# First layer's end on two engines: GpSimd finishes three heads while VectorE divides

## What is computed

```
e = exp(leaky_relu(s_src[src] + s_dst[dst], 0.2))
rowsum = segment_sum(e, src)
agg = segment_sum(e[:, None] * h[dst], src)
h_prime = agg / rowsum[:, None]
outs.append(elu(h_prime))        # once per head, four heads
x = x + mean(outs)
```

## Time and profile before

| | us |
|---|---|
| median of 3 runs | 4261.27 (4261.18 to 4268.39) |
| the profiled execution, device time | 4261.19 |
| its span in the trace | 4258.6 |
| VectorE busy over the span | 2922.2 |
| GpSimd busy over the span | 1967.2 |
| this stage, first of VectorE's wide instructions to the next layer's first | 1654.1 to 1828.1 |

### The profile page before, as it was taken

One profiled execution on the slowest core, in us unless ns is written; L12 is line 12 of the kernel. 1 busy time (PEld: TensorE's weight loads), 2 busy tenths in 40 slices (PEclk: granted clock), 3 DMA queues, 4 the chain that ended last, 5 costly groups with the idle time before them and its releaser, 6 DMA issues. The chain is left out here.

```text
span 4258.6 us, 43791 instructions
## 1 busy us (share of the span) xinstructions
PE 1503.5 (35%) x10631; PEld 933.2 (22%) x10631; DVE 2922.2 (69%) x5610; ACT 1413.3 (33%) x3645; POOL 1967.2 (46%) x2324
## 2 busy tenths in 40 slices
PE   3270201110000000000565541322221498999988
PEld 2150101110000000000222220111111386444444
DVE  5875599984678888988887866577878677132131
ACT  1442402111366567533011212344444553010011
POOL 0047778736777760002677771677777230000000
PEclk9995555555555555555887775555555799999999
DMA  3000000005776760000233332688887275868845
GB/s 143 16 21 1 4 1 1 1 1 157 200 196 190 196 170 0 0 0 19 60 91 101 101 91 60 208 258 261 257 260 236 61 204 180 331 225 277 279 144 194
DMA packets 215402, 553.60 MB, mean 130 GB/s; under 512 B 46178, under 2 KB 112412, under 8 KB 214405
## 3 DMA queue, kind: packets, MB, share of 16 engines
q0 software_dynamic: 99984, 272.83, 23.1%
q1 hardware_dynamic: 115188, 278.18, 19.2%
HBM read 485.70 MB, written 65.20 MB: 129 GB/s over the span
## 5 line engine op out<-in xcount | busy, mean ns | idle before, releaser
L2898 PE MATMUL fourth_bank<-fourth_tile,fourth_z 128*128 128x512 f16 (+1 forms) x2800 | 559.7, 362 | 19.8 <-DVEq L3059 10.1
L2257 POOL DMA_INDIRECT heads_got<-rec,heads_slot x416 | 482.3, 1159 | 134.7 <-issue 88.4
L1778 POOL DMA_INDIRECT sum_got<-rec,sum_slot x416 | 437.7, 1052 | 132.6 <-issue 68.8
L1103 POOL DMA_INDIRECT table<-edges_record,edges_place x391 | 419.8, 1074 | 123.7 <-POOL table_pause L264 107.4
L1374 POOL DMA_INDIRECT blend_got<-rec,blend_slot x416 | 401.9, 966 | 136.1 <-issue 123.7
L1474 PE MATMUL blend_count<-blend_mov,blend_stat 128*128 x1100 | 288.7, 406 | 231.6 <-DVE blend_stat L1429 213.3
L218 PE MATMUL edges_p_key<-kept_ident,edges_key_row 128*128 128x128 f32 x4 | 1.1, 427 | 981.6 <-DVEq L176 981.6
L2898 PEld LDWEIGHTS fourth_bank<-fourth_tile,fourth_z 128*128 128x128 f16 x2800 | 261.6, 99 | 311.6 <-issue 15.0
L1864 DVE TENSOR_TENSOR first_y<-first_y,sum_got 128x516 f32 x416 | 291.9, 702 | 33.3 <-DVE sum_got L1842 12.5
L2371 DVE TENSOR_TENSOR third_a_y<-third_a_y,heads_got 128x520 f32 x416 | 289.5, 696 | 1.3 <-DVE third_a_y L2371 0.2
L1428 DVE TENSOR_SCALAR blend_mov<-built_iota_low,built_low 128x800 f16 x550 | 248.7, 452 | 56.9 <-issue 47.9
(11 more groups left out here) (678 smaller groups left out, 4441.0 us busy)
## 6 DMA issues: line engine op xcount, KB each, us to landing
fourth_tile<-cs SPq DMA_DIRECT2D x100, 800.0 KB, 4.5
fourth_tile<-ct SPq DMA_DIRECT2D x100, 800.0 KB, 4.3
ct<-blend_cst SPq DMA_DIRECT2D x20, 1000.0 KB
heads_counts<-ct SPq DMA_DIRECT2D x25, 800.0 KB
cs<-heads_flipped SPq DMA_DIRECT2D x25, 800.0 KB, 5.4
attend_cnt<-ct SPq DMA_DIRECT2D x50, 256.0 KB, 3.0
sort_low_wide<-low SPq DMA_DIRECT2D x4, 3136.0 KB, 21.8
attend_cnt<-ct SPq DMA_DIRECT2D x25, 288.0 KB, 4.0
```

Of the source, the lines that this page charges most:

```text
L1103: pool.indirect_dma_start(table, bass.IndirectOffsetOnAxis(ap=K["place"][0:lanes, t:t + 1], axis=0), K["record"][0:lanes, t, :], None).the ...
L1778: pool.indirect_dma_start(got[:, t % (HELD * PART), :], None, rec_dram, bass.IndirectOffsetOnAxis(ap=slot[:, t:t + 1], axis=0)).then_inc(g ...
L2257: pool.indirect_dma_start(got[:, buf, r, :], None, rec_dram, bass.IndirectOffsetOnAxis(ap=slot[:, t:t + 1], axis=0)).then_inc(gathered[buf ...
L2898: last = pe.matmul(bank[m][:, 0:w], z2[s % 2][:, k, part, :], tile[:, n % RING, at:at + w], start=(k == 0 and part == 0), stop=(k == NB - ...
```

## The change

`finish_head` and the sum of heads 0 and 1 leave VectorE. GpSimd gets a block of its own in `finish_once`: for heads 0, 1 and 2 it waits for `lifted`, takes the maximum with zero in one instruction, adds `e` in a second, and behind head 1 it adds head 1 to head 0. Each of its instructions is awaited before the next. VectorE waits for `joined` and for `finished` once, ahead of the last head's three pieces. ScalarE's code is unchanged; its waits on `finished` are now for GpSimd.

```diff
-            def finish_head(k):
-
-                dve.wait_ge(lifted, k + 1)
-                step(dve.scalar_tensor_tensor(head(k), head(k), 0.0, e, ALU.max, ALU.add))
-                dve.sem_inc(finished, 1)
...
                 subtract_low(k)
                 correct(k)
-                if k >= 1:
-                    finish_head(k - 1)
-                if k == 2:
-                    step(dve.tensor_tensor(head(0), head(0), head(1), ALU.add))
+            dve.wait_ge(joined, 1)
+            dve.wait_ge(finished, heads - 1)
             for n, at in enumerate(thirds):
                 finish_last(n, at)
+
+        @block.gpsimd
+        def _(pool):
+            for k in range(heads - 1):
+                pool.wait_ge(lifted, k + 1)
+                pool.tensor_scalar(head(k), head(k), 0.0, None, ALU.max).then_inc(cut, 1)
+                pool.wait_ge(cut, k + 1)
+                pool.tensor_tensor(head(k), head(k), e, ALU.add).then_inc(finished, 1)
+                pool.wait_ge(finished, k + 1)
+                if k == 1:
+                    pool.tensor_tensor(head(0), head(0), head(1), ALU.add).then_inc(joined, 1)
+            pool.wait_ge(joined, 1)
```

More of the change, by code:

```diff
@@ L1897, in finish_once @@
         v, ready, estimated, split, products = (c.sem(n) for n in ("v", "ready", "estimated", "split", "products"))
-        subtracted, divided, lowered, lifted, finished = (c.sem(n) for n in ("subtracted", "divided", "lowered", "lifted", "finished"))
+        subtracted, divided, lowered, lifted = (c.sem(n) for n in ("subtracted", "divided", "lowered", "lifted"))
+        cut, finished, joined = c.sem("cut"), c.sem("finished"), c.sem("joined")
         x = K["x"][:, :, :]
```

## The result

The changed kernel takes 4291.76 us (median of 4 runs, 4289.76 to 4294.54) against 4261.23 for the kernel before (4 runs): ratio 1.0068, 95% interval 1.0051 to 1.0085, so 22 to 36 us slower. The forecast was 4284.1, range 4259 to 4302.

What follows compares the result with a forecast made beforehand. The stage was taken as one VectorE chain with its ScalarE helper ahead of it. GpSimd's holds of 37.3 us less 14.45 saved gave +22.85 us on the profiled 4261.19 or median 4261.27, forecast 4284.1, range 4259 to 4302.

Steps and rivals of the forecast that it cites:

- the step that decides: What VectorE does during GpSimd's instructions: each holds VectorE for its full length, 37.3 us in all; full hold 66%.
- the boundary forecast: Head 0's maximum on GpSimd waits for the VectorE instruction boundary at 1711.26, then runs to 1714.4.
- Head 2's hand-over: Head 2 lifted at about 1805, during head 3's high subtraction, some 26 us of VectorE's chain left; pair costs 10.1 us.
- The 14.45 us taken off the chain: Four instructions leave VectorE's chain in the stage: 3 x 3.64 + 3.53 = 14.45 us saved.
- The full length: VectorE's loss per GpSimd instruction, taken as that instruction's whole duration; lower end 0.07 us an instruction.
- The gather of 4.06 us: Earlier-stage GpSimd gather beside a two-input VectorE instruction, 4.06 us instead of 0.95; cited as evidence of the hold.
- No hold: Rival A: GpSimd runs beside VectorE for nothing, the whole 14.45 us is kept, 4246.8 us; chance 18%.
- a partial hold: Rival B: VectorE gets some turns between pieces of GpSimd's stream; at half of 37.3 us, +4.2, 4265.5; chance 12%.
- VectorE always wins the interface: Rival C: GpSimd waits until VectorE runs dry at head 3's low subtraction, then work is serial; 4285 us, chance 4%.
- The fourth rival: Rival D: a GpSimd instruction runs far slower than three passes; each further us on an addition costs 4; no chance given.
- the shortest cover of 15.7: From 1778.0 to 1793.7, 15.7 us for GpSimd's two instructions on head 2; a 10.1 us pair fits.
- The term that was mis-sized: GpSimd's instruction times: three maxima at 3.1 us and four additions at 7.0, 37.3 us in all.

Runs made afterwards that it cites:

- the first probe: Kernel before plus a block behind the first layer's end: GpSimd alone, then its additions beside five kinds of VectorE instruction; kernel time meaningless, VectorE stretched 13.4 us or nothing.
- the serial kernel: Changed kernel with VectorE told to wait while GpSimd works, so nothing overlaps but ScalarE: 4300.71 us, ratio 1.0083, stage 210.34 us.
- the probes: Two kernels, the kernel before plus a block timing GpSimd instructions, alone or also beside VectorE; maximum alone 8.31 us, multiply-and-add 2.86.

## Why the prediction was right, and where its size was off

**Mechanism.** Right in the step that decides: VectorE lost GpSimd's instructions nearly whole, seven times, and for head 0 at the boundary forecast (the maximum was granted at 1710.45; on the axis of before, 0.8 us later, that is the predicted 1711.26). GpSimd got its turn between VectorE instructions 0.03 us apart, and one VectorE instruction passed between two of GpSimd's. ScalarE never became late. Head 2's hand-over met the last high subtraction of head 3, as forecast, though 7.5 us later than 1805 because of the longer holds ahead of it. The 26 us of VectorE's chain said to be left there count in the pair's own hold; without it 15.7 us were left, still enough for both holds to count in full. The 14.45 us taken off the chain closed the sum of every experiment that had them.

The full length was a guess of the prediction's all the same, and the rows did not show it. The gather of 4.06 us was held by VectorE, but it did not hold VectorE: L553, which started 0.82 us before the gather ended, stands at 3.49 us. That GpSimd's arithmetic holds VectorE, and for how long, was first shown by the profile after. The Trainium skill (SBUF — State Buffer, Who interferes with whom) has the exclusion for the whole instruction and exempts VectorE instructions with one SBUF input outside the two-port mode; the first probe agrees with both halves, 13.4 us against nothing.

**Rivals.** No hold (4246.8) and a partial hold (4265.5) fell with the profile, and the serial kernel closed the matter: 2.94 us is all that overlap is worth. That VectorE always wins the interface fell too: VectorE never ran dry and has no idle time at head 3's low subtraction. The fourth rival wanted an instruction far slower than three passes, 8.9 us; none was, with 8.3 us at most. But the maximum came near that, and a pair took 8.16 + 6.8 = 15.0 us, just inside the shortest cover of 15.7. The sign hung on the hold alone.

**The term that was mis-sized** is what GpSimd's instructions take. The maximum was put at 3.1 us, by the rate of a select that reads and writes one stream, with 5.8 as upper end. It takes 8.15 to 8.3. By VectorE's stretches the three maxima cost 7.98 + 7.98 + 7.74 = 23.7 us instead of 9.3. The four additions cost 6.60 + 6.64 + 5.43 + 5.43 = 24.1 instead of 28: 7.0 was right for two of them (6.93 and 6.96 alone), two are of the quick pairing (5.86). Together 47.8 instead of 37.3 us, which puts the stage at +33.4 instead of +22.85. The row taken for the maximum was one stream in and out like it, but another operation; the probes show that on GpSimd the operation and even the pair of operations decide the time (2.86, 8.3 or 11.0 us for the same columns). Its slope was drawn through two selects of different types besides, 128x128 f32 and 128x512 f16. The bounds had small slips: IOTA's rate gives 2.98 us for 3200 columns, not 2.9, and twice 3.1 is 6.2, not 5.8; neither would have reached 8.

Luck had a part in the number. The two errors ran against each other, +14.4 us from the maxima and -3.9 from the additions. The 7.0 us of an addition had no row under it, only bounds of 3.1 and 8.9. And the range held by its slack: with the maximum at its upper end and the additions at 7.0 it would have ended at 4292.2, below the profiled 4294.54; it went on to 4300 and a little over because the additions were put at 9.0 as well, which none of them took.

## What to carry to other kernels

Before moving elementwise work from VectorE to GpSimd, look at what VectorE will run meanwhile: if it reads two SBUF tiles, or is of the kind that took 1.83 us here where others took 3.49 (L387, the constant addition), the move costs GpSimd's whole duration, but for some tenths of a microsecond, and saves VectorE's. Where VectorE is the chain that bounds the stage, the move then loses whenever GpSimd's instruction is the longer one, however much idle time GpSimd has. Put it beside reductions, fills or instructions with a PSUM input, or give the work to ScalarE, which here took twice VectorE's time for a product and still gained all of VectorE's, since it had the idle time for it. Look for this loss in the durations of single instructions, not among the waits, and read the price of a GpSimd instruction only from a row of the same operation.

## What the runs showed that was not expected

GpSimd's scalar instruction over 3200 float32 columns takes 8.3 us with one operation, 11.0 with two, but 2.86 when the two are multiply and add. Its addition of two tiles takes 5.52, 5.86 or 6.93 us by which tiles are paired.
